# Block numbers carried in registers over the rounds of the first edge loop, and decoded in pieces on TensorE

## What is computed

```python
past, future = edge_index                      # src, dst of each edge, sorted by dst in the input
fwd_in = concat([x[future], x[past], edge_attr])
bwd_in = concat([x[past], x[future], edge_attr])
flow_fwd = relu(relu(fwd_in @ W1f + b1f) @ W2f + b2f)
flow_bwd = relu(relu(bwd_in @ W1b + b1b) @ W2b + b2b)
fwd_agg = segment_sum(flow_fwd, future)        # sum over the edges of a node
bwd_agg = segment_sum(flow_bwd, past)
x = layernorm(x + mlp(concat([fwd_agg, bwd_agg])))
```

## Time and profile before

| what | value |
|---|---|
| median of 3 runs | 4364.2 us (4361.36 to 4403.15) |
| profiled execution | 4380.07 us, span 4378.4 us |
| PE, DVE, POOL, ACT busy over the span | 3028.9, 2496.1, 2045.1, 1472.7 us |
| mean granted TensorE clock | 0.903 of full speed |
| first edge loop (layer0_edges_phase) | about 945 to 2442 us of the span |
| idle of PE before L903, ended by the sequencer | 13.1 us |

### The profile page before, as it was taken

One profiled execution on the slowest core, in us unless ns is written; L12 is line 12 of the kernel. 1 busy time (PEld: TensorE's weight loads), 2 busy tenths in 40 slices (PEclk: granted clock), 3 DMA queues, 4 the chain that ended last, 5 costly groups with the idle time before them and its releaser, 6 DMA issues. The chain is left out here.

```text
span 4378.4 us, 114954 instructions
## 1 busy us (share of the span) xinstructions
PE 3028.9 (69%) x33069; PEld 2036.8 (47%) x33070; DVE 2496.1 (57%) x7775; ACT 1472.7 (34%) x3385; POOL 2045.1 (47%) x3286
## 2 busy tenths in 40 slices
PE   2420000057777787777777579999999968969998
PEld 1100000036666666666666345555555548962222
DVE  7841222366666666666666369899989955540000
ACT  0011111114333333333334267777777740000000
POOL 1047777724444444444444258888888850000000
PEclk9999999969888888988889689899989979989999
DMA  9101111134334444333443711011000130009673
GB/s 375 71 12 22 23 22 23 22 92 137 123 114 137 139 137 136 120 123 118 137 139 109 162 30 28 26 28 27 27 26 27 28 72 3 3 37 382 271 301 138
DMA packets 190546, 431.94 MB, mean 99 GB/s; under 512 B 32352, under 2 KB 143066, under 8 KB 177274
## 3 DMA queue, kind: packets, MB, share of 16 engines
q1 hardware_dynamic: 156988, 365.02, 23.8%
q0 software_dynamic: 32816, 61.65, 6.3%
q10 hardware_dynamic: 520, 2.80, 0.2%
HBM read 227.36 MB, written 136.86 MB: 83 GB/s over the span
## 5 line engine op out<-in xcount | busy, mean ns | idle before, releaser
L210 POOL DMA_INDIRECT sorted_edges<-s_record,s_index x400 | 475.1, 1188 | 370.6 <-issue 362.1
L811 POOL TENSOR_TENSOR e_part<-e_rest,e_part 128x256 bf16<-128x256 f32 x202 | 132.8, 658 | 789.2 <-ACT e_part L853 789.2
L1018 DVE TENSOR_TENSOR e_strip<-e_p_aw,e_strip 128x256 f32 x804 | 334.7, 416 | 270.4 <-issue 201.3
L1353 POOL TENSOR_SCALAR m_oh<-m_iotab,m_rec 128x128 bf16<-128x128 bf16 x812 | 472.3, 595 | 0.1
L2059 PE MATMUL r_p_o<-r_W,r_X 128*32 128x512 f32 (+1 forms) x1050 | 408.7, 550 | 40.5 <-DMA r_W<-dense_strips 38.3
L805 POOL TENSOR_TENSOR e_ohw<-e_oh,e_rec 128x512 bf16<-128x512 bf16 x408 | 420.2, 1057 | 10.4 <-DVE e_oh L995 7.8
L261 PE MATMUL s_p_t<-s_ident,s_oh_src 125*128 125x125 f16 x100 | 21.2, 284 | 503.5 <-issue 258.7
L844 ACT ACTIVATE e_hid<-e_p_hid,e_b 128x512 f32<-128x512 f32 x204 | 140.2, 687 | 565.0 <-PE e_p_hid L903 565.0
L1002 DVE TENSOR_SCALAR e_ohw<-e_p_iota,e_rec 128x128 bf16<-128x128 f32 x816 | 327.5, 402 | 0.0
L2059 PEld LDWEIGHTS r_p_o<-r_W,r_X 128*32 128x32 f32 x1050 | 114.3, 110 | 321.5 <-issue 282.4
L1515 PE MATMUL m_p_w<-m_w,m_h 64*128 64x256 f32 x1640 | 259.7, 440 | 0.0
(11 more groups left out here) (312 smaller groups left out, 7419.1 us busy)
## 6 DMA issues: line engine op xcount, KB each, us to landing
r_W<-dense_strips SPq DMA_DIRECT2D x18, 6400.0 KB, 17.8
e_strip<-e_zeros SPq DMA_DIRECT2D x26, 3200.0 KB, 13.8
dense_strips<-e_strip SPq DMA_DIRECT2D x25, 3200.0 KB
sorted_edges<-s_neg SPq DMA_DIRECT2D x1, 40560.0 KB, 161.4
e_rec<-sorted_edges POOLq DMA_DIRECT2D x208, 130.0 KB, 2.4
m_rec<-sorted_edges SPq DMA_DIRECT2D x208, 130.0 KB, 2.1
A<-dense_strips POOLq DMA_DIRECT2D x25, 800.0 KB, 28.0
sorted_edges<-s_record,s_index POOLq DMA_INDIRECT x400
```

The source lines that it names most:

```text
L210: pool.indirect_dma_start(dram["edges"], bass.IndirectOffsetOnAxis(ap=index[s][:, c:c + 1], axis=0), record[s][:, c, :], None).then_inc(s_ ...
L1018: i = V.tensor_tensor(at, p_aw[u][:, v, :].rearrange("p (k c) -> p k c", k=2), at, ALU.add)
L1353: i = g.tensor_scalar(oh[s][:, t, :], iotab[:, :], rec[s][:, t, CDST:CDST + 1], None, ALU.is_equal)
```

## The change

Three things change in the loop; no arithmetic on data does.

1. TensorE: `blocks_of` is split. The load and the source number are taken behind `second`, ahead of `sums`. Two target numbers are decoded at the slot's end behind `dense` (all four in slot 7), the other two in the next slot behind `turn`, ahead of `hidden`. Slot 7 now loads too; its five numbers go by moves into five registers that live over the rounds, and the next round's first slot takes them from there.
2. VectorE: both sets of numbers, `now` and `ahead`, are carried over the round's end in ten registers, put there by moves behind slot 7 and taken at the top. The two calls of `blocks_of` at the top of the round are gone, and slot 7 has one like the others. The weighted one-hots stay with the engines that they were with.
3. The eight semaphores `loaded` are allocated at the program's outermost level under another name, and are no longer cleared at the end of the phase.

```diff
--- before.py
+++ after.py
@@ -537,6 +537,37 @@
 
     return (block(packed >> (G * BITS)) if source else None,
             [block((packed >> (BITS * t)) & ((1 << BITS) - 1)) for t in range(G)] if targets else None)
+
+
+def packed_blocks(nc, engine, table, n, s):
+
+    return engine.value_load(table[0:1, bass.ds(body_of(nc, n, s), 1), TPACK[s % 2]], min_val=0, max_val=(1 << (G + 1) * BITS) - 1)
+
+
+def unpacked_block(nc, engine, packed, t):
+
+    value = (packed >> (BITS * t)) & ((1 << BITS) - 1) if t < G else packed >> (G * BITS)
+    return nc.snap(value, engines=[engine.engine], min_val=0, max_val=NB - 1)
+
+
+class Carried:
+
+
+
+    def __init__(self, nc, engine, name, count):
+        self.nc, self.engine = nc, engine
+        self.registers = [engine.alloc_register(f"{name}{k}") for k in range(count)]
+
+    def put(self, values):
+        for register, value in zip(self.registers, values, strict=True):
+            self.engine.reg_mov(register, value)
+
+    def take(self):
+        return [self.nc.snap(self.engine.snap(register), engines=[self.engine.engine], min_val=0, max_val=NB - 1) for register in self.registers]
+
+    def release(self):
+        for register in self.registers:
+            self.engine.free_register(register)
 
 
 def staged(n, j, *stages):
@@ -702,7 +733,7 @@
         p_aw = [ps(f"p_aw{i}", [P, 2, 2 * P]) for i in range(2)]
         p_iota = ps("p_iota", [P, 512])
 
-        loaded = [sem(f"loaded{s}") for s in slots]
+        loaded = dram["e_loaded"]
         w_chain, b_chain, p_set = sem("w_chain"), sem("b_chain"), sem("p_set")
         d_const, d_w, d_b, d_start, d_flush, d_zero = sem("d_const"), sem("d_w"), sem("d_b"), sem("d_start"), sem("d_flush"), sem("d_zero")
         prime = sem("prime")
@@ -948,18 +979,30 @@
 
             def work(n, j, blocks):
                 staged(n, j, (turn, 5))
+                if blocks:
+                    src, packed, dsts = blocks
+                    dsts = dsts + [unpacked_block(nc, pe, packed, t) for t in range(len(dsts), G)]
                 if j + 4 >= 0:
-                    hidden(*group(n, j + 4), blocks)
-                later = blocks_of(nc, pe, table, *group(n, j + 5)) if j + 5 >= 0 and j + 1 < U else None
-                staged(n, j, (second, 3), (sums, 1), (dense, 2))
-                return later
-
+                    hidden(*group(n, j + 4), (src, dsts))
+                staged(n, j, (second, 3))
+                more = j + 5 >= 0
+                if more:
+                    packed = packed_blocks(nc, pe, table, *group(n, j + 5))
+                    src = unpacked_block(nc, pe, packed, G)
+                staged(n, j, (sums, 1), (dense, 2))
+                return (src, packed, [unpacked_block(nc, pe, packed, t) for t in range(2 if j < U - 1 else G)]) if more else None
+
+            carried = Carried(nc, pe, "blocks", G + 1)
             blocks = None
             for j in range(-AHEAD, 0):
                 blocks = work(1, j, blocks)
+            carried.put([blocks[0]] + blocks[2] + [unpacked_block(nc, pe, blocks[1], t) for t in range(len(blocks[2]), G)])
             with pe.Fori(1, round_end(last), U) as n:
+                first = carried.take()
+                blocks = (first[0], None, first[1:])
                 for j in slots:
-                    blocks = work(n, j, blocks if j else blocks_of(nc, pe, table, *group(n, 4)))
+                    blocks = work(n, j, blocks)
+                carried.put([blocks[0]] + blocks[2])
 
         @block.vector
         def _(dve):
@@ -1052,18 +1095,22 @@
                     if j + 4 >= 0:
                         weigh_hi(*group(n, j + 4), t)
                 staged(n, j, (one_hots, 7))
-                later = blocks_of(nc, dve, table, *group(n, j + 2)) if j + 2 >= 0 and j + 1 < U else None
+                later = blocks_of(nc, dve, table, *group(n, j + 2)) if j + 2 >= 0 else None
                 staged(n, j, (cut_rest, 3))
                 return later
 
-            ahead = None
+            carried = [Carried(nc, dve, name, G + 1) for name in ("now", "ahead")]
+            now, ahead = None, None
             for j in range(-AHEAD, 0):
-                ahead = work(1, j, None, ahead)
+                now, ahead = ahead, work(1, j, None, ahead)
+            for held, blocks in zip(carried, (now, ahead)):
+                held.put([blocks[0]] + blocks[1])
             with dve.Fori(1, round_end(last), U) as n:
+                now, ahead = ((held[0], held[1:]) for held in (c.take() for c in carried))
                 for j in slots:
-                    now = ahead if j else blocks_of(nc, dve, table, n, 0)
-                    ahead = later if j else blocks_of(nc, dve, table, *group(n, 1))
-                    later = work(n, j, now, ahead)
+                    now, ahead = ahead, work(n, j, now, ahead)
+                for held, blocks in zip(carried, (now, ahead)):
+                    held.put([blocks[0]] + blocks[1])
     clear(nc, used)
 
 
@@ -2130,6 +2177,7 @@
     }
     with ExitStack() as ctx:
         dram["sent"] = [ctx.enter_context(nc.semaphore(f"sent{k}")) for k in range(2)]
+        dram["e_loaded"] = [ctx.enter_context(nc.semaphore(f"e_loaded{s}")) for s in range(U)]
         dram["a_loaded"] = ctx.enter_context(nc.semaphore("a_loaded"))
         sort_phase(nc, io, dram, io["sort_consts"])
         with ExitStack() as inner:
```

## The result

The changed kernel takes 4206.1 us in the median of four runs (4180.7 to 4208.1), the kernel before 4371.5 in the same session. The ratio is 0.961, with an interval of 0.957 to 0.965. The forecast was 4263 us in a range of 4195 to 4335: the sign and the range hold, and the gain is 165 us where the sum said 101.

The account below looks back on a forecast made before the run. No engine is full; TensorE's waits bound the loop, chiefly 217.3 us on its own sequencer before `second`. Slots 90 us less, slot 7 8 more, VectorE's round ends 19 less: 101 less, 4263 us, range 4195 to 4335.

Parts of the forecast that it names:

- round's end: VectorE's two loads and ten decoded numbers go, moves come: 19 us less, bounds 17 us worse to 70 better.
- slot 7: TensorE's last slot of a round, previously without a load, gets one: 0.3 us each, 8 us more.
- The gap and its place: TensorE's gap before `second` is one `blocks_of`, 1.8 us of sequencer work; its load fits behind `second`, ahead of `sums`.
- the mean of 0.6 us: Saving per slot in slots 1 to 6: 0.7 at full clock, up to 0.5 at partly half clock; 90 us less.
- all gaps close: Rival: 165 us less in the slots, TensorE also granted the full clock more often; 4195 us, chance 0.15.
- Pieces: TensorE decodes two targets behind `dense`, two behind `turn`, 0.44 us each; no hole opens at once, but the lead shrinks.
- sequencer-bound after all: Rival: TensorE's sequencer work per slot stays, holes reappear among `hidden`'s matmuls, only the round's end gains; 4350 us, chance 0.13.
- the moves: VectorE's register moves around its loop's jump, priced at 0.07 to 0.1 us apiece, 1.4 to 2.9 us in all.
- Even: TensorE's round end: load and five numbers (2 us) go, four targets and moves come; no net gain.
- The collision: Rival: moves delay VectorE's jump fetch behind the zeroing transfer, 3 to 4 us per round end; 4355 us, chance 0.09.
- VectorE resumes over 4 us after the jump: At VectorE's round end: a sign that would show the prediction wrong.
- PE loses its loop: Rival: some 15 added instructions push TensorE's loop out of instruction memory, forcing fetches every round; 4500 us, chance 0.05.

Follow-up runs that it names:

- carry_no_split: Changed kernel, but TensorE loads and decodes all five numbers in one go between `hidden` and `second`, where they were; 4375.0 us, 1.002 of the kernel before.
- extra_load: Changed kernel with the block-number load and its bound check repeated once per slot between `turn` and `hidden`; 4346.8 us, 0.994 of the kernel before.
- whole_behind_second: Changed kernel, but TensorE loads and decodes all five numbers in one go behind `second`; 4169.5 us, 0.953 of the kernel before.
- dve_alone: Kernel before with only VectorE's loop as changed, TensorE's loop as before; 4345.0 us, 0.994 of the kernel before.
- pe_alone: Kernel before with only TensorE's loop as changed, VectorE's loop as before; 4261.8 us, 0.973 of the kernel before.
- before_aligned: Kernel before with VectorE's loop shifted by 40 fulfilled waits, so it lies in three fetch pieces; 4329.6 us, 0.988 of the kernel before.
- write_later: Changed kernel with SyncE's write-out of a finished strip waiting for three groups more; 4178.6 us, 0.957 of the kernel before.

## Why the prediction was right, and where its sizes were off

Per round, in the prediction's terms, against the table (25 rounds):

| term | forecast | measured |
|---|---|---|
| slots 2 to 6 | 5 x 0.6 x 25 = 75 less | 5 x 0.97 x 25 = 121 less |
| slots 0 and 1: slot 1's 0.6 (15) and the round's end (19) | 34 less | 2.90 x 25 = 72 less |
| slot 7 | 8 more | 1 less |
| TensorE's first edge loop | 101 less | 194 less |
| untouched stages | 0 | 22 more |
| whole execution | 101 less | 172 less |

**The gap and its place.** Right. The wait ahead of `second` was one `blocks_of`, the room between `second` and `sums` took it, and no wait of that size came in another place. carry_no_split shows it from the other side: with the numbers left where they were, nothing is gained.

**The size per slot.** The count of the sequencer's work gave 5.75 us for a slot; it is 5.62, and extra_load shows that it is the sequencer's. The step that failed is the next one, the mean of 0.6 us: "In a slot that ran partly at half clock the gap was 0.53 us and the engine is the limit; it can give back up to 0.5." It took the clock of those slots as given. Before, slots 2 to 6 took between 6.44 and 7.5 us; now they take 5.55 to 5.77. The granted clock of the loop rose from 0.88 to 0.94, and the slot shown above is at 1.00. A slot of 6.47 us gave 0.85, more than the 0.7 counted, and a half-clock slot gave over 1 us instead of under 0.5. The weight was off too: the mean of 0.6 counts as many slots of the second kind as of the first, and of the 120 slots 2 to 6 only 19 took over 6.8 us. The rival "all gaps close", at 4195 us, held this rise and nothing else that was missing, and the result is nearest to its number. Its reason against, the count of 5.75 us, was sound as a count and still no bound on the mean.

**Pieces.** They were priced as part of the gain, and are none of it: whole_behind_second reaches the same slot without them. By the count the sequencer's work is the same in either order, so this could have been said ahead. The rival "sequencer-bound after all" was right that the slot is the sequencer's and wrong that the slot doesn't shrink.

**Slot 7.** 8 us were set aside for its new load; it costs nothing that shows, as its mean went from 5.68 to 5.63. Where the load isn't behind `second` it costs 1.5 us (carry_no_split).

**Round's end.** The mis-sized term is the moves. They were priced one by one at 0.07 to 0.1 us, 1.4 to 2.9 us in all; the ten before the jump are one step of 0.23 us, and with the reading back (0.30) they come to about half a microsecond. VectorE's idle time fell by 2.7 us, near the upper bound of 2.9, though the jump grew by 0.8. The reason given for taking only 0.8 us, that a sooner VectorE just waits longer for the second piece, is a real mechanism: in dve_alone, carry_no_split and extra_load the hole grew to as much as 3.2 us. It did not act in the changed kernel, because there the zeroing is issued 2.5 us behind the jump and the second piece comes in time; the mean hole fell from 0.5 us to nothing. The prediction took the time of issue (0.5 us behind the jump, in the round it read) as fixed, and in that it failed. That the gain came out near its upper bound instead of being eaten as in carry_no_split was not foreseen. "Even" for TensorE's own round end was wrong: its gaps in slot 0, 1.80 us before `turn` and 1.94 before `second` in the mean of all rounds, are 0.95 and 0 now, with 0.5 new before `sums`. It loses the load of about 1 us and gets no full price for the moves. That this lies ahead of the wait for VectorE and gives nothing by itself held: slots 0 and 1 of pe_alone take 20.88 us, no less than before.

**The collision.** It exists, but not as priced. The first fetch meets the write-out, not the zeroing, and comes 0.8 us later, not 3 to 4. The second fetch is the one that goes with the zeroing, and it does come some 3 us later where that is issued right behind the jump; the changed kernel is spared this by the time of issue. The test "VectorE resumes over 4 us after the jump" came close, at 3.6.

**PE loses its loop.** No. TensorE's loop is 1559 instructions in the trace, 7 more than before, and queue 8 has no fetch from 1031 to 2250 us.

**What was given back.** The sum counted nothing in stages that the change doesn't touch. The layer-1 edge loop took 1012 us before and 1026 after (columns as in the earlier trace rows); before:

```profile
2553.00:3565.00 1012.00, 947.00 (x9357) 556.32 (x9356) 924.00 (x2634) 760.64 (x1835) 865.03 (x2030) 0.91 0.10 26
```

and after:

```profile
2358.00:3384.00 1026.00, 962.40 (x9345) 562.44 (x9346) 924.11 (x2632) 760.21 (x1835) 864.29 (x2029) 0.89 0.10 26
```

VectorE does the same 924 us, TensorE's clock is lower, and the next stage took 9.5 us more at a clock of 0.94 instead of 0.97. Over the kernels of this study the layer-1 loop, the same code in all, took 982 to 1027 us, with no order by what was changed in the first loop. So I read this one as spread of the granted clock from one execution to the next and not as an effect of the change; no run settles it. It is also what blurs comparisons under 1% here. The next stage does show an order: it took 288 to 290 us at a clock of 0.97 to 0.98 in the three kernels whose TensorE loop is as before (before, dve_alone, before_aligned), and 295 to 301 us at 0.94 to 0.95 in the eleven whose TensorE carries its numbers, carry_no_split with its unchanged time among them. That looks like an effect of the change on code that it doesn't touch, of about 8 us; its cause stays open.

**The rule on fetching.** The Trainium skill, "Runtime: NRT & Kernel Launch", section Instruction fetch mechanics, says that a taken branch outside the instruction memory's window forces a fetch. The trace agrees, 2.8 to 3.7 us on VectorE. The same section gives most engines room for 512 instructions in blocks of 16 KiB; VectorE's fetches here are 8.2 KB each (0.97 MB in 119), which would be 128 instructions by the section's 256 to 16 KiB (an estimate), and a loop of 369 instructions stays in only when it lies in three such pieces. The measurement decides.

## What to carry to other kernels

Put register loads and decoding on TensorE's queue where its engine has long matmuls ahead of it, and count a slot as the sum of its sequencer's steps. A row without idle time before it doesn't prove that the engine is the limit: compare the matmuls' pace with their register steps. When gaps close, count the slots that ran at the lower clock as well. Before shortening what an engine does at the end of a loop, look whether its fetch queue is busy in every round, and which large transfer is issued just behind the jump: the time saved can come back as a hole (2.5 us per round in carry_no_split). Where the loop begins can be worth as much as what it does (42 us here in the old kernel, 86 in the new one).

## What the runs showed of the hardware that was not expected

- VectorE's loop of 369 instructions: 5 fetches and 3.6 us of jump per round when it lies across four pieces, no fetch and 0.2 us in three. Why four pieces don't fit was not tested; five fetches per round for four pieces would suit a piece fetched ahead that pushes out the one needed next.
- VectorE's second fetch of a round came 7.7 to 8.0 us behind the jump where the 3.2 MB zeroing was issued 0.3 to 0.6 us behind it, mostly 4.5 to 5.0 where it was issued 1.7 us behind it or later (dve_alone), and 3.6 with no large transfer there (write_later). No run moved the zeroing alone.
- A register load from on-chip memory took TensorE's sequencer 0.29 us, and mostly 0.9 to 1.2 us beside a 3.2 MB transfer, wherever that transfer was put.
- Ten moves between registers that follow each other ran as one step of 0.23 us on VectorE's sequencer.
- Twelve matmuls whose weights are addressed by a register took 1.44 us when each followed its own register step, and 0.83 us where the sequencer was ahead.
